# Queue order of the first batches, the place of the list products, and the last tile of a cross-attention and expert kernel

## The reference

```python
x = x + tanh(g_xattn[0]) * attention(layernorm(x), ctx, ctx, ...)   # 16 heads of 16
x = x + tanh(g_ffn[0]) * ffn(layernorm(x), ...)
def ffn(x, ...):
    scores = softmax(xf @ w_router)                    # 8 experts
    weights, experts = top_k(scores, 2)
    h = silu(xf @ w1[e]) * (xf @ w3[e]);  y = h @ w2[e]
    shared = silu(xf @ ws1) * (xf @ ws3) @ ws2
    return shared / 3 + (sum of weight * y over the two experts) * 2 / 3
```

## Time and profile before

| | us |
|---|---|
| median of three runs | 862.77 |
| lowest, highest | 859.28, 864.61 |
| the profiled execution | 863.41 |
| its span, first to last instruction | 861.5 |

### The profile page before, as it was taken

The page is one execution under the profiler, slowest core; times in us unless marked ns, Lnnn a source line. Parts: engine busy times, 40 slices in busy tenths (PEclk is TensorE's granted clock), DMA queues, the critical chain, the costliest instruction groups (busy, mean ns, idle before and its releaser), DMA issues.

```text
span 861.5 us, 19377 instructions
## 1 busy us (share of the span) xinstructions
PE 793.5 (92%) x7106; PEld 708.7 (82%) x7107; DVE 532.3 (62%) x1086; ACT 408.3 (47%) x684; POOL 422.3 (49%) x461
## 2 busy tenths in 40 slices
PE   4659999899999998897999999999999999999996
PEld 4546777677777775567999999999999999999995
DVE  7846888799998979847464333333333333346785
ACT  5337776667766667552235333333333333342321
POOL 6623436566666644357554375646646572235000
PEclk9959999999999999999999999999999999999998
DMA  6644555765556554243377342414332412118531
GB/s 221 226 154 160 173 174 195 247 198 197 196 199 201 184 181 137 84 158 105 126 230 266 109 140 74 119 52 127 100 89 76 120 49 71 52 56 336 182 98 49
DMA packets 100525, 127.35 MB, mean 148 GB/s; under 512 B 17648, under 2 KB 82416, under 8 KB 100464
## 3 DMA queue, kind: packets, MB, share of 16 engines
q1 hardware_dynamic: 86320, 80.37, 29.4%
q0 software_dynamic: 14144, 46.19, 15.7%
HBM read 75.36 MB, written 50.91 MB: 147 GB/s over the span
## 4 chain that ended last, share of the span: by engine, by line
PE 76%; DVE 8%; DMA 6%; issue 3%; ACT 3%; POOL 2%; SPq 2%; ACTq 0%; DVEq 0%; POOLq 0%
PE bank L530 9%; PE bank L532 8%; PE bank L531 8%; PE bank_sm L530 5%; PE bank_ss L530 5%; PE bank_ss L531 5%; PE bank_ss L532 5%; PE bank_sm L531 5%; PE bank_sm L532 5%; PE bank_ss L585 5%; PE bank L614 4%; PE bank_sm L598 3%; DVE row_max L1174 3%; PE bank L621 2%; DMA qk_d<-qk_s 2%
## 5 line engine op out<-in xcount | busy, mean ns | idle before, releaser
L1174 DVE TENSOR_REDUCE row_max<-bank_sm 128x4 f32<-128x1024 f32 x124 | 151.6, 1222 | 55.0 <-PE bank_sm L598 53.2
L892 ACT ACTIVATE probs_T<-bank_ss 128x1024 f32<-128x1024 f32 x123 | 126.1, 1025 | 32.3 <-PE bank_ss L585 32.1
L1153 DVE TENSOR_TENSOR gT_l<-gg,gT_h 128x1024 fp32r<-128x1024 f32 x50 | 67.5, 1350 | 89.5 <-ACT gT_h L1015 89.4
L530 PE MATMUL bank<-w_h,gT_h 128*128 128x256 f32 x400 | 114.8, 287 | 6.9 <-DVE gT_l L1153 3.7
L530 PE MATMUL bank_ss<-xg_h,w_h 128*128 128x256 f32 x400 | 116.6, 291 | 0.0
L530 PE MATMUL bank_sm<-xg_h,w_h 128*128 128x256 f32 x400 | 113.4, 283 | 1.4 <-DVE xg_l L1153 1.3
L531 PE MATMUL bank<-w_h,gT_l 128*128 128x256 f32 x400 | 114.4, 286 | 0.0
L532 PE MATMUL bank<-w_l,gT_h 128*128 128x256 f32 x400 | 114.1, 285 | 0.0
L532 PE MATMUL bank_ss<-xg_l,w_h 128*128 128x256 f32 x400 | 113.3, 283 | 0.0
L531 PE MATMUL bank_ss<-xg_h,w_l 128*128 128x256 f32 x400 | 113.3, 283 | 0.0
L532 PE MATMUL bank_sm<-xg_l,w_h 128*128 128x256 f32 x400 | 112.9, 282 | 0.0
(11 more groups left out here) (177 smaller groups left out, 2023.0 us busy)
## 6 DMA issues: line engine op xcount, KB each, us to landing
qk_d<-qk_s SPq DMA_DIRECT2D x64, 256.0 KB, 3.8
w_raw<-wall POOLq DMA_DIRECT2D x27, 512.0 KB, 3.9
k<-qk_d SPq DMA_DIRECT2D x48, 256.0 KB, 3.9
q<-qk_d SPq DMA_DIRECT2D x48, 256.0 KB, 4.6
xg<-xs_d SPq DMA_DIRECT2D x35, 257.0 KB, 2.8
y_pairs<-y_d POOLq DMA_DIRECT2D x16, 512.0 KB, 9.5
x<-x SPq DMA_DIRECT2D x16, 256.0 KB, 4.7
c_s<-ctxT SPq DMA_DIRECT2D x16, 256.0 KB, 3.0
```

The costliest lines, as they stand in the source:

```text
L530: pe.matmul(out, ah, bh, start=first and k == 0, stop=False)
L892: act.activation(pT[:, 2 * (pv % 4):2 * (pv % 4) + 2, :].rearrange("p h t -> p (h t)"), exp_bank(V.b, pv)[:, :], ACT.Exp, scale=D ** -0.5) ...
L1153: return v.tensor_tensor(dst, ps, high.bitcast(F32), ALU.subtract)
L1174: v.tensor_reduce(mx[B.slot][:, :, :].rearrange("p t (r q) -> p r t q", r=2)[:, :, :, p], max_bank(B.b, p)[:, :].rearrange("p (r t k) -> p ...
```

## The change

- SP's order for the first three batches is written out. The max rows of batch 0 are issued ahead of the q terms of batch 2, and the q terms of batch 0 behind the k stores of batch 1. From iteration 0 on `one(i)` has the same order as before but for early x loads.
- `clear_q` and `clear_k` of the second and third buffer move from DVE to ACT; each buffer has its own semaphore.
- root takes its exponent from a tile of its own and doesn't wait for the constants; in the first iteration the context's rest comes behind it, and xnT_h one step earlier.
- The products of the token lists move from `positions` to `list_slots`, one iteration later. mask, mask_total and the two constant matrices of `rank` become fp32r.
- The three loads of the first weights are spread over three iterations; POOL's subtraction in `cut` is made in two halves; `add_bias` of the last two batches comes in iteration 15; `g_low(0)` comes ahead of `residual(x15)`.
- The last tile's hidden width is treated in halves: both up projections of a half, then silu, product and split of that half, with tiles of its own (in the free weight buffers) and two free banks for `down`. The routed results of the last batch are added ahead of `down`'s, and each 128 rows are stored by themselves.

```diff
-        acc = sb(keep, "mask_total", [P, TC, NX])
+        acc = sb(keep, "mask_total", [P, TC, NX], F32R)
+        counters = sb(keep, "counters", [P, 2, P], F32R)
...
+            def max_rows(C):
+                sp.wait_ge(mT_ok, C.n(1, 1))
+                for par in range(2):
+                    row = ROWS * par + MROW
+                    sp.dma_start(q4[C.slot][row:row + 1, :, :].bitcast(F32), mT[8 * par:8 * par + 8, :].bitcast(F32)).then_inc(mrow, 16)
...
             def one(i):
                 X, Eb, A, F, C, S2, S3 = (stage(i, k) for k in (5, 4, 3, 2, 0, -2, -3))
-                if C:
-                    sp.wait_ge(mT_ok, C.n(1, 1))
-                    for par in range(2):
-                        row = ROWS * par + MROW
-                        sp.dma_start(q4[C.slot][row:row + 1, :, :].bitcast(F32), mT[8 * par:8 * par + 8, :].bitcast(F32)).then_inc(mrow, 16)
-                if X and 1 < X.b < RX:
-                    load_x(X)
+                if C and C.b > 0:
+                    max_rows(C)
                 if Eb and Eb.b > R:
                     load_c(Eb)
-                if i == -AHEAD:
-                    load_c(X)
                 if S3:
                     store_turned(S3)
-                if F:
-                    moved(sp, ss_ps, F.n(PAIRS, -(R - 1) * PAIRS))
-                    if not among_first(F, R):
-                        terms_in(F, 1)
-                        terms_in(F, 0)
+                if F and not among_first(F, R):
+                    sp.wait_ge(ss_ps, F.n(PAIRS, -(R - 1) * PAIRS))
+                    terms_in(F, 1)
+                    terms_in(F, 0)
                 if A:
                     half_out(A, 1)
-                    if among_first(A, R):
-                        terms_in(A, 1)
-                if A and among_first(A, R - 1):
-                    load_c(X)
                 if S2:
                     store_x2(S2)
-                if X and not among_first(X, RX):
+                if X:
                     load_x(X)
                 if A:
                     half_out(A, 0)
-                    if among_first(A, R):
-                        terms_in(A, 0)
...
-            iterations(sp, one)
+            b0, b1, b2 = (Batch(k) for k in range(R))
+            load_c(b1)
+            load_x(b2)
+            half_out(b0, 1)
+            terms_in(b0, 1)
+            load_c(b2)
+            half_out(b0, 0)
+            load_x(Batch(3))
+            half_out(b1, 1)
+            terms_in(b0, 0)
+            load_c(Batch(3))
+            half_out(b1, 0)
+            terms_in(b1, 1)
+            load_x(Batch(4))
+            terms_in(b1, 0)
+            half_out(b2, 1)
+            terms_in(b2, 1)
+            half_out(b2, 0)
+            max_rows(b0)
+            terms_in(b2, 0)
+            for i in range(NB):
+                one(i)
...
-            for j in range(NB - 2, NB + 1):
+            for j in range(NB - 2, NB):
                 for b in mixed_at(j):
                     store_out(b)
+            for t in range(TS):
+                sp.wait_ge(last_mix, t + 1)
+                sp.dma_start(out[(NB - 1) * TR + t * P:(NB - 1) * TR + (t + 1) * P, :], o_o[(NB - 1) % 2][:, t, :]).then_inc(last_st, 16)
             sp.wait_ge(o_st[0], 16 * (NB // 2))
-            sp.wait_ge(o_st[1], 16 * (NB // 2))
+            sp.wait_ge(o_st[1], 16 * (NB // 2 - 1))
+            sp.wait_ge(last_st, 16 * TS)
...
             def rank(S3, at):
                 pe.wait_ge(oh_ok, S3.n(1, 1))
                 moved(pe, acc_ok, S3.n())
-                ones, upper = K[:, C_ONE:C_ONE + P], K[:, C_UP:C_UP + P]
+                if among_first(S3, 1):
+                    pe.wait_ge(count_ok, 1)
+                upper, ones = counters[:, 0, :], counters[:, 1, :]
...
+            with pe.Fori(end + 1, end + (NB - 1 - EARLY)) as g:
                 tile(g, SHARED, SHARED, routed=False)
-            down(end + (NB - 1 - EARLY), SHARED)
+            final = end + (NB - 1 - EARLY)
+            pe.wait_ge(xl_ok, final + 1)
+            pe.wait_ge(sg_ok, final)
+            pe.wait_ge(g_ok, final)
+            for n in range(2):
+                for ps, off in ((psH1, 0), (psH3, W3O)):
+                    for f in (2 * n, 2 * n + 1):
+                        r = three(ps[n][:, f % 2 * TR:(f % 2 + 1) * TR],
+                                  lambda k: (w_h[SHARED][:, off + k * HID + f * P:off + k * HID + (f + 1) * P],
+                                             w_l[SHARED][:, off + k * HID + f * P:off + k * HID + (f + 1) * P]),
+                                  lambda k: (xg_h[:, k, :], xg_l[:, k, :]), EC)
+                r.then_inc(last_up, 1)
+            down(end + (NB - 2 - EARLY), SHARED)
+            for n in range(2):
+                pe.wait_ge(last_gl, n + 1)
+                for t in range(TS):
+                    r = three((psX, psH1[0])[t][:, t * E:(t + 1) * E],
+                              lambda k: (fin_h[:, 2 * n + k, t * P:(t + 1) * P], fin_l[:, 2 * n + k, t * P:(t + 1) * P]),
+                              lambda k: (w_h[SHARED][:, W2O + (2 * n + k) * E:W2O + (2 * n + k + 1) * E],
+                                         w_l[SHARED][:, W2O + (2 * n + k) * E:W2O + (2 * n + k + 1) * E]), 2, first=n == 0, last=n == 1)
+                    if n == 1:
+                        r.then_inc(last_w2, 1)
...
+            def clear_k(i):
+                act.activation(k4[i][:, :, :], K[:, C_MROW:C_MROW + 1].unsqueeze(2).to_broadcast([P, H // 2, L]), ACT.Copy).then_inc(k_init[i], 1)
+            def clear_q(i):
+                act.activation(q4[i][:, :, :], zero[:, 0:1].unsqueeze(2).to_broadcast([P, H // 2, L]), ACT.Copy).then_inc(q_zero[i], 1)
+            act.wait_ge(zero_ok, 1)
...
-                    if p == 3 and A:
+                    if p == (2 if A and A.b == 0 else 3) and A:
                         from_bank(xnT_h, T0, xnT_ps, A, q_ps, A.n(2), xnTh_ok)
...
+                        if Eb.b == 2:
+                            clear_q(1)
...
+                if A and among_first(A, R - 1):
+                    act.wait_ge(k_in, 16)
+                    clear_k(A.b + 1)
+                if A and A.b == 1:
+                    clear_q(2)
...
+                    act.activation(counters[:, :, :].rearrange("p n q -> p (n q)"), K[:, C_UP:C_UP + 2 * P], ACT.Copy).then_inc(count_ok, 1)
...
+            act.wait_ge(g_ok, end + (NB - 1 - EARLY))
+            for n in range(2):
+                act.wait_ge(last_up, n + 1)
+                act.activation(sg[:, 2 * n:2 * n + 2, :].rearrange("p f t -> p (f t)"), psH1[n][:, :], ACT.Silu).then_inc(last_sg, 1)
+                act.wait_ge(last_g, n + 1)
+                act.activation(fin_h[:, 2 * n:2 * n + 2, :], gg[:, 2 * n:2 * n + 2, :], ACT.Copy).then_inc(last_gh, 1)
...
             def positions(S3, at):
                 v.wait_ge(rk_ps, S3.n(1, 1))
                 v.tensor_tensor(pos[:, :, :], at.rearrange("p (t e) -> p t e", t=TC),
                                 K[:, C_EB:C_EB + NX].unsqueeze(1).to_broadcast([P, TC, NX]), ALU.add).then_inc(pos_ok, 1)
+            def list_slots(S3):
                 v.wait_ge(pos_ok, S3.n(1, 1))
-                mark(v.tensor_tensor(pr[:, :, :, :], oh[:, :, :, :], pos[:, :, :].unsqueeze(2).to_broadcast([P, TC, 2, NX]), ALU.mult))
-            def list_slots(S3):
-                settle()
+                link(v.tensor_tensor(pr[:, :, :, :], oh[:, :, :, :], pos[:, :, :].unsqueeze(2).to_broadcast([P, TC, 2, NX]), ALU.mult))
...
                 if A and among_first(A, R - 1):
-                    clear_q(A.b + 1)
-                    clear_k(A.b + 1)
                     clear_v(A.b + 1)
...
             masks(x14)
+            g_low(0)
             residual(x15)
             residual_stats(x15)
             residual_variance(x15)
             positions(x14, rk_tail)
             list_slots(x14)
-            g_low(0)
             x_low_shared(2, 2)
...
-                gated(end + (j - EARLY))
-                g_low(end + (j - EARLY))
+                    gated(end + (j - EARLY))
+                    g_low(end + (j - EARLY))
+                else:
+                    v.wait_ge(gl_ok, end + (j - EARLY))
+                    for n in range(2):
+                        v.wait_ge(last_up, n + 1)
+                        v.wait_ge(last_sg, n + 1)
+                        v.tensor_tensor(gg[:, 2 * n:2 * n + 2, :].rearrange("p f t -> p (f t)"),
+                                        sg[:, 2 * n:2 * n + 2, :].rearrange("p f t -> p (f t)"), psH3[n][:, :], ALU.mult).then_inc(last_g, 1)
+                        v.wait_ge(last_gh, n + 1)
+                        low(fin_l[:, 2 * n:2 * n + 2, :], gg[:, 2 * n:2 * n + 2, :], fin_h[:, 2 * n:2 * n + 2, :]).then_inc(last_gl, 1)
...
-            add_late(NB - 1)
-            for b in mixed_at(NB):
-                mix(b)
+            b = NB - 1
+            v.wait_ge(yg_in[b], 16)
+            for k in range(2):
+                for t in range(TS):
```

(31 more changed lines are left out.)

33 lines of the change are left out of this document (17 added, 16 removed).

## The result

The changed kernel takes 838.01 us (median of 4 runs, 836.42 to 839.76), the kernel before 861.02 us on the same chip (4 runs, 858.8 to 864.61). The ratio is 0.9729, with a 95% interval of 0.9686 to 0.9773: 2.7% faster. The prediction was 834 us, in a range of 825 to 843.

A forecast was written before the change was run, and what follows sets the result against it. TensorE, busy 92% of the span, was taken as the bound, so its waits were to be won. Terms of 9.3, 4.4, 2.4, 3.4, 7.1, 2.6 and 0.3 gave 29.5 off 863.4: 834 us, range 825 to 843.

The forecast's parts named there:

- The ramp: 0 to 55 us: batch 0's max row, issued earlier by SP, shortens PE's stall; gain 9.3 us, bounds 6 and 12.
- batch 0's own delay: Ramp: q terms behind batch 1's later k stores put batch 0's scores 0.8 us later than before.
- The iteration: Iterations 4 to 11: moving products removes PE's 0.64 us wait at pair 6, 0.1 given back; 4.4 us in all.
- rank: Two rank matmuls in fp32r halve their 0.44 us: 0.22 us saved in 13 iterations and tail ranks; 2.4 us.
- rival B: Iterations: norm's second half waits behind leave_low, each gives only 0.2 us; 837, or 840 with the tail's stall; chance 0.17.
- The loads: First weight loads, one per iteration instead of three together: 3.8 us gained less 0.4 for issuing ahead of root; 3.4 us.
- The turn: Attention to experts: PE's waits of 0.89 and 3.69 us go, less low clock, shorter xg_l; 7.1 us (3.5 to 9).
- PE at half clock for longer: Sign that the prediction is wrong: PE stays at half clock for longer after the ramp's new start; no size given.
- The last tile: End of the kernel: with halves PE doesn't wait before the last down; gain 2.6 us (1.5 to 4.5).
- A: The ramp is held elsewhere, by ScalarE's clears ahead of k and q; it gives 4 rather than 9: 839; chance 0.14.
- D: Slower: products at pair 1 make slot_i late, so PE waits for xn in each iteration; over 871; chance 0.03.
- E: No change: SP's order is no bound, the ramp gives nothing, half the other 20 fails; 853 to 862; chance 0.03.

The follow-up runs named there:

- max row last: Changed kernel with batch 0's max rows issued behind batch 2's q terms in SP's order, not ahead of them; 841.5 us.
- biases as before: Changed kernel with add_bias of batches 14 and 15 again behind the last scatter of batch 12, after the iterations; 837.0 us.
- products back: Changed kernel with the products of the token lists again behind the positions, ahead of the residual's variance; 846.1 us.

## Why the prediction came out where it did

**The ramp: right in its mechanism, 9.3 us priced, 7.35 measured.** The queue's order was the stall: the row no longer stands in it, and with the max row last 3.5 of the 8.4 us at its issue are lost again. I had named the place of the row; that the stores leave when they are ready is by the traces the larger part, 4.9 us, and no run tests it. The term that was mis-sized is batch 0's own delay. I had put it at 0.8 us; the first scores were 2.0 us late. The price of the clears on ScalarE was right (1.93 to 1.98 us each for "at most 2.0"), but they are not what matters: with them on DVE the ramp is the same. The rest is PE's clock: from the first scores to the turned maxima it took 12.96 us in this execution, at a mean granted clock of 0.79, and 12.06 us at 0.86 in the one of the kernel with the biases as before, whose mark 1 is 63.32 (before the change 12.05 at 0.86). Over the nine executions of the same ramp mark 1 has a mean of 64.2, a gain of 7.5. I named a range of 6 to 12.

**The iteration: right, too small.** I had 0.55 us for the stall and 0.22 for rank in iterations 4 to 11; 1.11 were measured in each of 8 to 11 (21.27 to 20.16). Two steps were off. The norm gives nothing back, since leave_low waited for ACT and came 0.44 us behind it; rival B, which had it lose, did not come in the plain iterations. And the matmuls behind the wait had been slow, 0.50 us for a group that else takes 0.40; that went with the wait. The pieces do not add as I added them: alone, the faster rank widens the stall (21.5 us).

**rank: right.** Half of the 0.44 us: 0.22 in each iteration with the type alone changed. In the second stretch that is 1.5 us, since it gives nothing in iterations 4 to 6; the 2.4 us of the sum had the tail too, where no mark resolves it. The Trainium skill, "FP8 and Floating Point Precision", section TensorE Precision Notes, counts four passes for true fp32; three quarters saved, 0.33 us, is not what these runs show for a matmul of 16 columns, where the records go from four to two.

**The loads: 3.4 us priced, 1.7 measured between the two kernels, 2.3 by undoing it.** The saving of 3.8 us was there. The step that failed is the 0.4 us that I took off "for 0.6 us of issuing ahead of root in three iterations". It cost about 1.9 (2.38 less the 0.44 that iteration 4 has without a load). I had let the root be 0.6 us late and asked what is late by 0.6; I did not ask what the norm meets at its new time. The Trainium skill, "SBUF — State Buffer", section Who interferes with whom, says that the one of the two that comes second is blocked in full until the first is done. The trace agrees: leave_low ends at 180.99, the norm's first instruction at 181.15. Here that is 0.97 us (1.70 against 0.73), for being 0.08 us behind. This is rival B after all, in iterations 5 and 6 by the load ahead of the root, and in iteration 4 with or without it.

**The turn: 7.1 us priced, 4.15 measured** (4.0 with the mean of the seven executions of this code, 144.2)**.** The waits of 0.89 and 3.69 us went, and PE waits 0.35 us for xg_l in place of 1.30 (0.95 saved, 1.1 priced). Behind the rank of batch 13 these terms gave 9.3 us in this profile, more than the 7.1 priced; 5.2 us were lost ahead of it. (Over the seven executions it takes 66.1 to 69.4 us from mark 13 to that rank and 74.9 to 80.6 from there to the eighth gT_l, against 63.92 and 84.29 in the one of before.) What failed is the step that moves the biases to iteration 15 and counts only what they free. POOL gets there while DVE is in iteration 14, and I did not look at what DVE does then. The row stood in the trace of before: its norm took 2.24 us there beside one add_bias. That costs PE 2.4 us of waiting, and its clock after it. "PE at half clock for longer" was named among what would make the prediction wrong, for the ramp; it came here.

**The last tile: 2.6 us priced, 3.0 measured** over that stretch.

**The rivals.** A fell in its mechanism. B happened in iterations 4 to 6. D, slower, did not: the products at pair 1 delay nothing, since POOL still stands idle 4.92 us ahead of its leave_low in iteration 8. E did not.

## What to carry to other kernels

When an operation is moved on one engine, look up in the trace what the other engine of the port that DVE and POOL share does at the new time, not only what stands behind it in its own queue: 0.65 us of issue became 1 us of blocked norm, and two free-looking additions cost 2.4 us and 10 us of lower clock. If an engine runs ahead where its work thins out, hold it with a wait on what it must not meet; that one line, with a better gap for the rest, gave 8.5 us, a third of the whole change. And take the gains of a stage by marks that both traces have, since totals here hid 1.5 us effects under 3 us of scatter elsewhere.

## What the runs showed of the hardware

- A blocked DVE operation does not get in between POOL operations that follow each other without a pause, the issue of an indirect DMA among them. The norm of iteration 14 started 0.51 us into such an issue and stood through it and three add_bias (3.71 us, norm 4.67); where no add_bias followed the issue, the same norm took 0.86. The addition to mask_total stood through an issue and two add_bias (3.18 us for 0.17).
- Who wins the port was decided by tenths. The norm is two instructions of 0.41 us, the second 0.32 us behind the first. With leave_low 0.44 us behind its start it took 0.73 us; with leave_low 0.15 us behind, the second instruction waited (1.71); with leave_low 0.08 us ahead, the first did (1.70).
- PE's clock after a wait differed between executions for the same wait. After 4.06 us idle at the end of iteration 14 the changed kernel ran at a granted 0.50 for two windows of 5 us; the kernel with products back had the same 4.06 us wait and was at full speed 4 us later (its sixteen matmuls of `values` took 1.51 us and then 1.07, against 1.94 and 1.93). Over the six executions with the same code from mark 13 to the rank, the time goes with the mean granted clock: 66.55 us at 0.92, 66.52 and 67.62 at 0.90, 69.10 and 68.68 at 0.85, 69.37 at 0.83.
- Mark 1 moves by 3 us between executions with the same ramp, and goes with the mean granted clock from 0 to the mark: 63.18, 63.32 and 63.59 us at 0.92; 63.98, 64.01, 64.09 and 64.29 at 0.89; 64.75 at 0.87; 66.25 at 0.85. The first scores start within 0.5 us in all nine (29.42 to 29.96).
